# Router logits with the router weights as the standing operand in sliding slices, and the class token's value column copied by ScalarE

## The reference

```python
# 1 mixer: x (32, 64, 256, 4) -> h (32, 256, 256)
q, k, v = proj(Wq), proj(Wk), proj(Wv)
ew, ek = exp(w_bias * local_mask), exp(k)
y = sigmoid(q) * einsum('ts,nsd->ntd', ew, ek * v) / einsum('ts,nsd->ntd', ew, ek)
h = layernorm(y @ out_w + out_b + flatten(x)) * ln_g + ln_b
# 2 attention: a class token in front, so 257 tokens of 256 channels, 16 heads of 16
h = concat([cls_tok, h])
h = h + holo_attention(layernorm(h))     # each projection: 32 resonances, then amp * cos(phase)
# 3 feed-forward: a shared expert (1024 hidden) and 8 routed ones (256 hidden), two per token
xf = layernorm(h).reshape(-1, 256)                      # 32 * 257 = 8224 tokens
shared = silu(xf @ shared_w1.T) * (xf @ shared_w2.T) @ shared_w3.T
scores = sigmoid(xf @ router_w.T)                       # the router logits: 8 per token
top_idx = top_k(scores + expert_bias, 2)
gates = scores * one_hot(top_idx).sum(-2)
h = h + shared + sum over experts of gates * w3 @ (silu(w1 x) * (w2 x))
```

## Time and profile before

| | |
|---|---|
| three runs | 2208.34, 2207.89, 2204.55 us; median 2207.89 |
| profiled execution | 2204.59 us, span 2202.8 us, mean granted clock 0.99 |
| PE busy | 2081.1 us (94%), 15678 matmuls |
| PEld busy | 1847.7 us (84%) |
| DVE busy | 1436.8 us (65%), 3061 instructions |
| ACT busy | 991.9 us (45%), 2044 instructions |
| POOL busy | 684.3 us (31%), 737 instructions |
| logits L1586 | 390 matmuls, 1.9% of the span on the chain of waits |
| copies L863 | 32, DVE busy 60.1 us in them |

### The profile page before, as it was taken

The page is one execution under the profiler, slowest core; times in us unless marked ns, Lnnn a source line. Parts: engine busy times, 40 slices in busy tenths (PEclk is TensorE's granted clock), DMA queues, the critical chain, the costliest instruction groups (busy, mean ns, idle before and its releaser), DMA issues. The chain is left out here.

```text
span 2202.8 us, 42583 instructions
## 1 busy us (share of the span) xinstructions
PE 2081.1 (94%) x15678; PEld 1847.7 (84%) x15678; DVE 1436.8 (65%) x3061; ACT 991.9 (45%) x2044; POOL 684.3 (31%) x737
## 2 busy tenths in 40 slices
PE   5899999999999999999889999999999999999998
PEld 4677777787887877777758999989998888889998
DVE  7677777777777877777644444677754444445666
ACT  2155555455555555554553333322225555554332
POOL 4334334233243343342202111000013333333665
PEclk9999999999999999999999999999999999999999
DMA  2533433424334233344214343000013333334665
GB/s 76 84 66 64 85 62 77 81 54 89 70 65 85 66 73 82 62 80 71 50 39 155 120 135 130 27 23 30 30 44 99 106 104 104 106 103 121 183 182 157
DMA packets 125274, 189.25 MB, mean 86 GB/s; under 512 B 23153, under 2 KB 76418, under 8 KB 125074
## 3 DMA queue, kind: packets, MB, share of 16 engines
q1 hardware_dynamic: 101232, 134.65, 26.0%
q0 software_dynamic: 12736, 34.69, 5.6%
q10 hardware_dynamic: 11106, 17.19, 2.4%
HBM read 84.32 MB, written 49.58 MB: 61 GB/s over the span
## 5 line engine op out<-in xcount | busy, mean ns | idle before, releaser
L675 ACT ACTIVATE pT<-ps 128x514 f32<-128x514 f32 x512 | 304.9, 597 | 308.7 <-PE ps L485 304.0
L842 DVE TENSOR_REDUCE mx<-ps 128x2 f32<-128x512 f32 x512 | 340.7, 680 | 106.1 <-PE ps L468 106.0
L2001 POOL DMA_INDIRECT z<-zd,itab x136 | 128.3, 944 | 470.2 <-DVE itab L1914 253.5
L468 PE MATMUL ps<-km,q 112*128 112x256 f32 x1024 | 246.0, 327 | 16.3 <-DMA km<-klo 10.5
L485 PE MATMUL ps<-q,km 114*128 114x258 f32 x1024 | 228.7, 305 | 31.5 <-ACT pT L675 31.5
L485 PEld LDWEIGHTS ps<-q,km 114*128 114x128 f32 x1024 | 159.1, 189 | 81.0 <-ACT pT L675 54.3
L1291 PE MATMUL ps<-zhi,whi 128*128 128x256 f32 x1056 | 218.4, 289 | 2.5 <-issue 2.4
L468 PEld LDWEIGHTS ps<-km,q 112*128 112x128 f32 x1024 | 166.7, 191 | 58.3 <-issue 24.9
L1291 PE MATMUL ps<-zhi,wlo 128*128 128x256 f32 x1056 | 214.7, 285 | 0.0
L1291 PE MATMUL ps<-zlo,whi 128*128 128x256 f32 x1056 | 213.9, 284 | 0.0
L1319 ACT ACTIVATE sil<-ps 128x512 f32<-128x512 f32 x132 | 79.0, 598 | 264.6 <-PE ps L1291 264.6
(11 more groups left out here) (320 smaller groups left out, 4997.5 us busy)
## 6 DMA issues: line engine op xcount, KB each, us to landing
yd<-raws SPq DMA_DIRECT2D x136, 128.0 KB, 1.8
q<-qhi SPq DMA_DIRECT2D x128, 129.0 KB, 4.1
km<-khi SPq DMA_DIRECT2D x256, 64.5 KB, 3.2
xs<-in_x SPq DMA_DIRECT2D x64, 256.0 KB, 4.4
z<-hscr SPq DMA_DIRECT2D x46, 256.0 KB, 2.9
raws<-in_wu SPq DMA_DIRECT2D x12, 768.0 KB, 4.8
hscr<-h SPq DMA_DIRECT2D x34, 256.0 KB, 5.1
zd<-z SPq DMA_DIRECT2D x33, 256.0 KB, 2.0
```

The source lines that it names most:

```text
L468: last = pe.matmul(ps[:, i % 2, k * L:(k + 1) * L], q2[p % U][0:MAXROW, QAT[g], t * P:(t + 1) * P], km[p % 2][0:MAXROW, k, g, 0:L], start= ...
L675: act.activation(pT[:, 2 * g:2 * g + 2, t, :], ps[:, score_bank(b, n):score_bank(b, n) + 2, 0:N], ACT.Exp, scale=HD ** -0.5).then_inc(s_ok, 1)
L842: dve.tensor_reduce(mx[:, t, 2 * QAT[g]:2 * QAT[g] + 2], ps[:, i % 2, :].rearrange("p (k l) -> p k l", k=2), AX_X, ALU.max, negate=True).t ...
L2001: pool.indirect_dma_start(zg(i), None, zd_rows, bass.IndirectOffsetOnAxis(itab[:, i:i + 1], 0)).then_inc(zg_in[i % NG], 16)
```

## The change

Logits. The router weights now stand in PE and the tokens stream. A tile `rww` of 240 columns per channel half is zero but for 16 columns in its middle: 8 rounded weights and 8 of their rest. A slice of 128 columns of it puts these 16 at any multiple of 16, so up to 8 token blocks add up in one PSUM tile of 128 rows and 256 tokens, each in 16 rows of its own. A block takes four matmuls of 256 columns (hi and lo tokens, two channel halves). The 33 blocks form five groups, of 7, 8, 8, 8 and 2. After a group ACT copies its tile to SBUF, PE transposes it in two pieces into bank 7, and DVE adds the two halves of each logit into `raw_lg`, from which one tanh is taken, in unit 2 of round 8. The router weights are loaded into a corner of `acc`.

Class column. The copy of column CLS moves from `normalise` on DVE to ACT (`keep_class`), behind the copy of the last group of the image's values. Three semaphores of the set-up that followed one another become one, with counts 1 to 3.

```diff
+        def keep_class(b):
+            act.wait_ge(og_ok, b * G + G)
+            act.activation(clso[:, :, bass.ds(b, 1)], og[:, :, CLS:N], ACT.Copy).then_inc(clso_ok, 1)
@@ step of ACT in stage A
                     if n == 0:
                         take_group(b - 1, G - 1)
+                        keep_class(b - 1)
@@ normalise on DVE
-            if t == LT - 1:
-                dve.tensor_copy(clso[:, :, bass.ds(b, 1)], og[:, :, CLS:N]).then_inc(clso_ok, 1)
@@ stage B, tiles
-    rwr = sb("rwr", [P, FT * NE])
-    rwh = sb("rwh", [P, FT, NE], F32R)
-    rwl = sb("rwl", [P, FT, NE], F32R)
+    RW = 2 * NE
+    LEFT = P - RW
+    rww = sb("rww", [P, FT, LEFT + P], F32R)
+    hits = [sb("hit%d" % c, [P, K * LT * NE]) for c in range(TOP)]
+    one = [t[:, 0:WIDE] for t in hits]
+    rwr = acc[:, 1, 0:FT * NE].rearrange("p (f e) -> p f e", f=FT)
+    GROUPS = (X1 + 1) // 2
+    members = [[] for g in range(GROUPS)]
+    for k in range(X1):
+        xs = ([NX * k - 1] if k > 0 else []) + ([NX * k, NX * k + 1] if NX * k < EXTRA else [])
+        members[k // 2] += [k] + [X1 + j for j in xs]
+    LOGITS_AT = [(2 * g + 2, 0) for g in range(GROUPS - 1)] + [(X1 - 1, 1)]
+    LOGITS_OUT = [(2 * g + 1, 3) for g in range(GROUPS - 1)] + [(X1 - 1, 0)]
+    raw_lg = hits[0]
+    lgT = one[1][:, 0:L]
@@ PE
             def logits(k, p):
-                for t in range(LT if k < B else 1):
-                    at = (k * LT + t) * NE
-                    dst = ps[:, 5, at:at + NE] if at < BANK else ps[:, 7, 0:NE]
-                    mm = [(z_, w_, f) for z_, w_ in ((zhi, rwh), (zlo, rwh), (zhi, rwl)) for f in range(FT)]
-                    for n, (z_, w_, f) in enumerate(mm):
-                        last = pe.matmul(dst, z_[p][:, f, t * P:(t + 1) * P], w_[:, f, :], start=(n == 0),
-                                         stop=(n == len(mm) - 1))
+                g = next(g for g in range(GROUPS) if k in members[g])
+                at = LEFT - RW * sorted(members[g]).index(k)
+                if k == members[g][0] and g > 0:
+                    pe.wait_ge(lgc_ok, g)
+                mm = [(z_, f) for z_ in (zhi, zlo) for f in range(FT)]
+                for n, (z_, f) in enumerate(mm):
+                    last = pe.matmul(ps[:, 5, 0:L], rww[:, f, at:at + P], z_[p][:, f, :],
+                                     start=(n == 0 and k == members[g][0]),
+                                     stop=(n == len(mm) - 1 and k == members[g][-1]), skip_group_check=True)
+                if k == members[g][-1]:
+                    last.then_inc(lg_ps, 1)
+            def turn_logits(g):
+                pe.wait_ge(lgc_ok, g + 1)
+                if g > 0:
+                    pe.wait_ge(lge_ok, g)
+                for t in range(LT):
+                    last = pe.transpose(ps[:, 7, t * P:(t + 1) * P], lgT[:, t * P:(t + 1) * P], eye[:])
                 last.then_inc(lg_ps, 1)
@@ PE, unit (k, u), after output
+                    if (k, u) in LOGITS_AT:
+                        turn_logits(LOGITS_AT.index((k, u)))
@@ ACT
+            def copy_logits(g):
+                act.wait_ge(lg_ps, 2 * g + 1)
+                act.activation(lgT, ps[:, 5, 0:L], ACT.Copy).then_inc(lgc_ok, 1)
@@ ACT, end of unit (k, u), after weights
-                    if k == X1 - 1 and u == 1:
-                        act.wait_ge(lg_ps, K)
+                    if (k, u) in LOGITS_OUT:
+                        copy_logits(LOGITS_OUT.index((k, u)))
+                    if k == X1 - 1 and u == 2:
+                        act.wait_ge(lge_ok, GROUPS)
                         act.wait_ge(w_lo, NU)
-                        act.activation(sc[:, 0:BANK], ps[:, 5, :], ACT.Tanh, scale=0.5).then_inc(th_ok, 1)
-                        act.activation(sc[:, BANK:WIDE], ps[:, 7, 0:NE], ACT.Tanh, scale=0.5).then_inc(th_ok, 1)
+                        act.activation(sc, raw_lg[:, 0:WIDE], ACT.Tanh, scale=0.5).then_inc(th_ok, 1)
@@ DVE
+            def gather_logits(g):
+                dve.wait_ge(lg_ps, 2 * g + 2)
+                order = sorted(members[g])
+                runs = [[k for k in order if k < X1], [k for k in order if k >= X1]]
+                for run in runs:
+                    j, n = order.index(run[0]), len(run)
+                    for t in range(LT):
+                        m = n - 1 if t == 1 and run[-1] == B else n
+                        if m > 0:
+                            cols = raw_lg[:, run[0] * LT * NE:(run[0] + m) * LT * NE].rearrange("p (b t e) -> p b t e", t=LT, e=NE)
+                            last = dve.tensor_reduce(
+                                cols[:, :, t, :],
+                                ps[:, 7, t * P + RW * j:t * P + RW * (j + m)].rearrange("p (b s e) -> p b e s", s=2, e=NE),
+                                AX_X, ALU.add)
+                last.then_inc(lge_ok, 1)
@@ DVE, start of stage B
+            dve.memset(rww[:].bitcast(F32), 0.0)
             dve.memset(ones[:].bitcast(F32), 1.0).then_inc(rt_step, 1)
@@ DVE, end of unit (k, u), before route
+                    if (k, u) in LOGITS_AT:
+                        gather_logits(LOGITS_AT.index((k, u)))
```

More of the change, by code:

```diff
@@ L175, in stage_a @@
     clso = sb("clso", [P, G, B])
-    (c_load, c_set, d_step, half_ok, mask_ok, wb_ok, ew_ok, arg_ok, cos_ok, w_ok, clsvar_ok, clsrs_ok, clsz_ok, clsT_ps,
-     clsT_ok, clsr_ps, clsr_ok, clsqkv_ps, spread_ok, mix_in) = (
+    (c_load, c_set, d_step, half_ok, mask_ok, wb_ok, ew_ok, arg_ok, cos_ok, w_ok, clsvar_ok, clsrs_ok, clsz_ok, cls_ps,
+     clsT_ok, clsr_ok, spread_ok, mix_in) = (
         sem(x) for x in ("c_load", "c_set", "d_step", "half_ok", "mask_ok", "wb_ok", "ew_ok", "arg_ok", "cos_ok", "w_ok",
-                         "clsvar_ok", "clsrs_ok", "clsz_ok", "clsT_ps", "clsT_ok", "clsr_ps", "clsr_ok", "clsqkv_ps",
+                         "clsvar_ok", "clsrs_ok", "clsz_ok", "cls_ps", "clsT_ok", "clsr_ok",
                          "spread_ok", "mix_in"))
@@ L608, in _ @@
             last = pe.matmul(ps[:, 6, f:f + 1], clsz[:, f * P:(f + 1) * P], one1[:], start=True, stop=True)
-        last.then_inc(clsT_ps, 1)
+        last.then_inc(cls_ps, 1)
         pe.wait_ge(clsT_ok, 1)
@@ L612, in _ @@
             last = pe.matmul(ps[0:3 * HARM, 5, 16:17], basT[:, f, :], zT[:, f, CLS:N], start=(f == 0), stop=(f == FT - 1))
-        last.then_inc(clsr_ps, 1)
+        last.then_inc(cls_ps, 1)
         pe.wait_ge(clsr_ok, 2)
@@ L620, in _ @@
         pe.matmul(ps[0:NH, 7, 0:D], rbc[:], Wz[:, 2, :], start=True,
-                  stop=True).then_inc(clsqkv_ps, 1)
+                  stop=True).then_inc(cls_ps, 1)
         filler(5, 12)
@@ L757, in _ @@
         act.activation(tr[:], tn[:], ACT.Sin).then_inc(cos_ok, 1)
-        act.wait_ge(clsT_ps, 1)
+        act.wait_ge(cls_ps, 1)
         act.activation(zT[:, :, CLS:N], ps[:, 6, 0:FT].rearrange("p (f o) -> p f o", o=1), ACT.Copy).then_inc(clsT_ok, 1)
-        act.wait_ge(clsr_ps, 1)
+        act.wait_ge(cls_ps, 2)
         act.activation(rT[:, CLS:NP], ps[0:3 * HARM, 5, 16:17].broadcast_to([3 * HARM, 2]), ACT.Copy).then_inc(clsr_ok, 1)
@@ L992, in _ @@
         attn_stats(0, 0)
-        dve.wait_ge(clsqkv_ps, 1)
+        dve.wait_ge(cls_ps, 3)
         chain(dve.tensor_copy(clsh[:], ps[:, 4, 0:2 * FT].rearrange("p (n f) -> p n f", n=2)))
@@ L1188, in stage_b @@
     acc = sb("acc", [P, LT, D])
-    one = [sb("hit%d" % c, [P, WIDE]) for c in range(TOP)]
+    hits = [sb("hit%d" % c, [P, K * LT * NE]) for c in range(TOP)]
+    one = [t[:, 0:WIDE] for t in hits]
     key, tmp, sum_a, sum_b, sc = (raws[:, n * WIDE:(n + 1) * WIDE] for n in range(5))
@@ L1232, in stage_b @@
         sem(x) for x in ("rt_step", "hits_ok", "pos_ps", "pos_ok", "idx_ok"))
-    consts = [(rwr[:], a["routerT"]), (ebias[:], a["ebias"]), (pref[:], a["pref"]), (rowid[:], a["rowid"]),
+    lgc_ok, lge_ok = sem("lgc_ok"), sem("lge_ok")
+    rwr = acc[:, 1, 0:FT * NE].rearrange("p (f e) -> p f e", f=FT)
+    consts = [(acc[:, 1, 0:FT * NE], a["routerT"]), (ebias[:], a["ebias"]), (pref[:], a["pref"]), (rowid[:], a["rowid"]),
               (tileid[:], a["tileid"]),
@@ L1367, in tile_turn @@
         if i == 1:
-            pe.wait_ge(th_ok, 2)
+            pe.wait_ge(th_ok, 1)
             pe.wait_ge(idx_ok, TOP)
@@ L1695, in _ @@
             act.wait_ge(b_load, 16 * (len(consts) + 1))
-            act.activation(rwh[:].rearrange("p f e -> p (f e)"), rwr[:], ACT.Copy).then_inc(r_hi, 1)
+            act.wait_ge(rt_step, 1)
+            act.activation(rww[:, :, LEFT:LEFT + NE], rwr, ACT.Copy).then_inc(r_hi, 1)
             act.activation(earlier[:], acc[:, 0, 0:P], ACT.Copy).then_inc(r_hi, 1)
@@ L1779, in keys @@
                 dve.wait_ge(w_lo, NU)
-                dve.wait_ge(th_ok, 2)
+                dve.wait_ge(th_ok, 1)
                 chain(dve.tensor_scalar(sc, sc, 0.5, 0.5, ALU.mult, ALU.add))
@@ L1943, in _ @@
             dve.wait_ge(r_hi, 2)
```

(3 more changed lines are left out.)

## The result

| | before | after |
|---|---|---|
| median of the runs | 2208.11 us (2204.55 to 2209.77, 4 runs) | 2174.70 us (2174.02 to 2176.61, 4 runs) |
| profiled execution | 2204.59 us | 2174.02 us, span 2172.2 |
| ratio | | 0.985, 95% interval 0.9835 to 0.9866 |

Faster by 33 us. The forecast was 2186.0 us, so 11 us of the gain had not been foreseen.

The account below looks back on a forecast made before the run. PE was taken to bound the logits stretch, and the attention stage where a change touches its short waits. Logits -26.0, clock -2.9, ScalarE's copy +7.0 sum to -21.9 us: 2186.0 from the median 2207.89, range 2174 to 2200.

Parts of the forecast that it names:

- Logits: Router logits on PE: 42.7 us removed, 16.7 us added, balance -26.0 us.
- the rival of the dear matmul: New logit matmuls on PE cost 0.236 us each instead of 0.118: -6.3 us, 2201.6; chance 0.04.
- The clock: Router logits stretch: two drops of PE's clock behind blocks of 24 logits go, counted as -2.9 us.
- Uncovered work: Router logits stretch: reductions, memset, copies and tanh on other engines stay hidden when PE shortens; 0 us.
- The class column, ScalarE: Attention stage: the copy behind og lengthens PE's wait for z by 0.24 us in 29 steps, +7.0 us.
- The class column, VectorE: Attention stage: 32 copies, 60.1 us, leave VectorE; worth 0, at most the rden wait of 10.2 us.
- the rival with VectorE released: Attention stage: VectorE's release takes PE's rden wait away, -32.1 us, 2175.8; chance 0.07.
- the clock is 1.00 from 1197 to 1386 us: Against the rival that the clock still drops in the logits stretch: -19.0 us, 2188.9; chance 0.12.
- ScalarE's copy costs 7 us and not 0: Against the rival that ScalarE's class copy costs nothing in the attention stage: -28.9 us, 2179.0; chance 0.12.
- no product of u = 1 waits for VectorE: Against the rival that VectorE becomes the bound in u = 0 of eight rounds: -8.3 us, 2199.6; chance 0.09.
- the copy on ScalarE lasts 0.21 us each time: Against the slower rival: attention stage copy held on ScalarE as on VectorE, 2.2 us a step, +35, 2243; chance 0.06.

Follow-up runs that it names:

- e8: Kernel before with each block of 24 logit matmuls parted into two of 12, same instructions: 2203.06 us, ratio 0.9987.
- e2: Kernel before with VectorE's class-column copy left out, a memset of one column in its place: 2206.19 us, ratio 1.0001.
- e1: Kernel before with only the class-column copy moved to ScalarE, behind og: 2214.04 us, ratio 1.0035.
- e4: Changed kernel with ScalarE's class copy in slot 5 of the step, behind z, instead of slot 0: 2165.07 us, ratio 0.9808 to the kernel before.
- e3: Kernel before, no instruction changed, with an unused 1728 B tile and wider hit tiles giving later tiles the changed kernel's places: 2189.09 us, ratio 0.992.
- e9: Kernel before with an unused tile of 64 B a partition behind rwl, moving the later tiles: 2193.85 us, ratio 0.9933.

## Why the prediction was right or wrong

**Logits: right.** By forecast 42.7 us leave PE and 16.7 come, -26.0. Counted from start to start of PE's instructions between the two marks, the logits took 41.45 us and now take 16.80 with their transposes, and the other transposes 1.07 less: -25.7. The new matmuls take 0.118 us each in most pieces and the transposes 0.11, as priced. A weight tile of mostly zeros costs what another does; the rival of the dear matmul fell.

**The clock: right in cause, a draw in size.** -2.9 us was read from two drops. The counts over fourteen kernels tie the drops to the blocks of 24, and e8's median, 3.7 us under before's, is near that price; but a profile of a kernel with such blocks holds 0 to 7 of them. That may also be why 25 runs of the kernel before spread over 14 us and ten of e8 over 7: the mean granted clock of each is known, 0.986 to 0.994 and mostly lower in longer runs for before, 0.990 to 0.994 for e8. It is argued, not shown: ten runs of e2, which has the blocks, spread over 8, and the kernel after, without them, has 0.988 to 0.993.

**Uncovered work: nearly right.** No reduction or copy makes PE wait in the rounds behind: the profile lists no wait of PE from 1220 to 1386 us. At the stage's start PE is idle 1.4 us more than before (187.57 busy of 189.00), which its waits of 1190 to 1220 us show in two:

```profile
PE ps L1307 <- issue: 1.0, 1, 1.0
PE ps L1307 <- POOL wlo L2084: 0.4, 1, 0.4
```

PE begins a round 0 whose first units are shorter, and meets GpSimd's low parts of the weights there. The profile finds no releaser for the longer wait, but it ends the same way: the kernel's hidden products wait for these low parts in round 0, and the two waits end at 1198.09 and 1204.35 us, right behind subtractions of GpSimd that end at 1197.94 and 1204.25. GpSimd's next subtraction runs over VectorE's norm of 3.85 us:

```profile
1205.32 3.92 DVE L1263 TENSOR_SCALAR z<-hb,mv,rs 128x256 f32<-128x256 f32 x2
1205.46 3.62 POOL L2084 TENSOR_TENSOR wlo<-raws,whi 128x1536 fp32r<-128x1536 f32 x1 [1.22 <-ACT whi L1718]
```

The same norm elsewhere takes 0.73 for the pair. The Trainium skill (VectorE: DVE Perf Modes, "Two Vector instructions with no wait between them") has VectorE's two-port modes share an interface with GpSimd; the two ends, 1209.24 and 1209.08, agree. Here, unlike for the class copy, the chain of waits runs through it, from VectorE into the transposes that PE starts at 1209.29. PE has other work nearly up to there, so it costs little: its last logits before end at 1209.20.

**The class column, ScalarE: right.** +7.0 us by forecast; 7.0 in the marks (9.5 in e1's), 7.1 in the z wait, 8.3 in e1's medians, whose interval of 0.17% to 0.53% (4 to 12 us) holds it. e4 takes it back by placing the same copy where ScalarE's queue has room.

**The class column, VectorE: right.** Worth 0, by e2, whose rden wait stays at 10.2 us.

**What failed: the list of costs had no term for where the tiles come to lie.** The change was taken for instructions alone. The diff shows the new size of `rww`; that the spacing of matmuls hangs on it no row of before could tell, as there all whole pieces of L1291 from 1200 us on, but for three of 4.3 to 4.4, take 2.84 to 2.96. e3 shows the term by itself: -9.9 us between positions and last output (after: -9.4), and in rounds 0 to 9 some 1.8 more (its -4.8 less the two drops of 1.5 that it happens not to have; an estimate). In the marks the account then closes: -26.0 - 2.9 - 1.8 + 1.4 = -29.3 in rounds 0 to 9, where -29.7 was measured. Left over are +1.5 us at both ends of the attention stage and of the span; the first L512 alone lies anywhere from 139.3 to 143.9 us in the kernels of this study.

The range was 2174 to 2200 us, and 2174.7 lies in it by 0.7 us. That is luck: its lower end allowed for the release of VectorE, which gave nothing, and the place of the tiles happened to give about as much.

**Rivals.** 2175.8 us, the rival with VectorE released, was closest to the time, and its mechanism is false: the rden wait is 10.2 us before, after and in e2. A time that fits shows no mechanism. The others fell too: the clock is 1.00 from 1197 to 1386 us, ScalarE's copy costs 7 us and not 0, no product of u = 1 waits for VectorE, the sliding matmul costs what L1307's do, and the copy on ScalarE lasts 0.21 us each time (0.218 at most), not 2.2.

## What to carry to other kernels

A tile that changes its size moves all tiles behind it: before a gain or loss in untouched stages is explained by waits, run the old kernel with an idle tile that restores the new places. Where PE is full, try idle tiles of 64 B between standing and streamed operands; here one of 64 B gave 15 us of 2209 (e9, 10 to 20 by the interval) and one of 1728 B 16.7 of 2206 (e3). A copy handed to another engine costs what it delays in that engine's queue, and what it frees at the giver is worth nothing where nobody waits for the giver, as here: put it behind the result that others wait for.

## What the runs showed of the hardware

- A matmul of 256 columns is spaced 0.118 us (2.84/24) or 0.113 (2.72/24) at the same granted clock of 1.00, by the distance of its two operands' places (for the hidden product). The Trainium skill (TensorE: Matmul & The Clock Gate, "Wait — 56ns, not 53.3ns?") gives columns divided by 2.4 GHz plus 2.5 ns, an estimate of 0.109 for 256; no run here reached it.
- The granted clock fell (mean 0.66 from 1214 to 1219 us before, between its levels of 1.2 and 2.4 GHz) right behind blocks of 24 matmuls of 8 columns each, though PE had no gap there. Over nine kernels with seven such blocks each, 25 of the 63 have a slow hidden product behind them, 0 to 7 in a kernel; behind blocks of 12 there is one, in e1, and none in e8.
- A VectorE operation that starts while a long GpSimd one runs can last until that one ends: 0.73 us for a pair of norms became 3.92 here, as the class copy had taken 2.25.
